# Attention's tail in another order: the last two reciprocal roots among GpSimd's scatters, row copies on ScalarE, the second image's norm ahead of the first's choice

## The reference, cut to what matters

```python
t = t + attn(layernorm(t))                     # 16 images x 256 tokens, 128 wide
z = layernorm(t)                               # per token
top_logits, top_idx = top_k(z @ Wg, 2)         # 8 experts
top_w = softmax(top_logits)
out = sum over e of combine[:, e] * (silu(z @ W1[e]) @ W2[e])
t = t + out
```

## Time and profile before

| what | value |
|---|---|
| median of 3 runs | 693.43 us (691.05 to 696.36) |
| profiled execution: span from first to last instruction | 692.4 us |
| busy share of the span: TensorE, VectorE, ScalarE, GpSimd | 85%, 69%, 45%, 38% |
| mean granted TensorE clock | 0.922 |
| last attention matmul of chunk 7 ends, first expert matmul starts | 475.8 us, 508.3 us |
| last scatter into the expert table issued, landed | 502.3 us, 504.6 us |

### The profile page before, as it was taken

How to read it: one execution, slowest core, us unless ns; L and a number is a source line. 1 busy time by engine, 2 the same in 40 slices (tenths; PEclk the granted TensorE clock), 3 DMA queues, 4 the chain that set the end, 5 groups by cost and what they waited for, 6 DMA issues and landing times. The chain is left out here.

```text
span 692.4 us, 11255 instructions
## 1 busy us (share of the span) xinstructions
PE 591.9 (85%) x3564; PEld 510.7 (74%) x3564; DVE 475.0 (69%) x1227; ACT 311.5 (45%) x619; POOL 264.6 (38%) x332
## 2 busy tenths in 40 slices
PE   5999999749789999999999998985259999999910
PEld 4788888636488998989898898885148888888810
DVE  6887784765558678777868788674527667767715
ACT  3322311243345353444535354442048888888800
POOL 4245334467000100141414132337603666666660
PEclk9999999959789999999999999877569999999975
DMA  7995155749450405050323314001178777766109
GB/s 265 360 336 171 39 172 169 242 163 341 133 149 5 153 1 153 2 172 13 124 62 98 88 43 142 25 17 47 39 250 290 240 238 229 259 230 212 60 5 359
DMA packets 55225, 105.49 MB, mean 152 GB/s; under 512 B 8744, under 2 KB 21689, under 8 KB 55040
## 3 DMA queue, kind: packets, MB, share of 16 engines
q1 hardware_dynamic: 50176, 96.24, 42.0%
q0 software_dynamic: 4992, 8.54, 3.5%
HBM read 58.15 MB, written 48.42 MB: 154 GB/s over the span
## 5 line engine op out<-in xcount | busy, mean ns | idle before, releaser
L1600 PE MATMUL bank<-rvx,s_expd 128*128 128x96 f32 x1024 | 136.1, 279 | 0.4 <-ACT s_expd L1052 0.4
L1600 PEld LDWEIGHTS bank<-rvx,s_expd 128*128 128x128 f32 x1024 | 129.7, 198 | 2.7 <-ACT s_expd L1052 2.0
L1904 POOL DMA_INDIRECT y_slots<-virt,pad_l x92 | 96.2, 1046 | 73.0 <-DVE virt L1955 50.0
L1052 ACT ACTIVATE s_expd<-bank 128x512 f32<-128x512 f32 x128 | 75.4, 596 | 96.6 <-PE bank L1584 96.0
L1247 DVE TENSOR_REDUCE s_max<-bank 128x2 f32<-128x512 f32 x128 | 87.2, 689 | 39.0 <-PE bank L1563 38.1
L968 POOL DMA_INDIRECT x_slots<-rows,slot_of x64 | 63.5, 993 | 58.6 <-DVE rows L1375 41.5
L934 POOL TENSOR_TENSOR ln_rstd<-ln_var,power 128x4 f32<-128x4 f32 x17 | 17.4, 1025 | 176.8 <-DVE ln_var L1223 176.8
L1943 DVE TENSOR_TENSOR k_stack<-virt,k_stack 128x512 fp32r<-128x512 f32 x92 | 63.5, 690 | 25.5 <-ACT k_stack L1923 24.8
L61 PE MATMUL bank<-pad_h,u_h 128*128 128x512 f32 x144 | 59.9, 416 | 8.2 <-DVE pad_l L399 8.2
L1584 PE MATMUL bank<-q_stack,k_stack 100*128 100x256 f32 x256 | 60.9, 321 | 5.2 <-DVE q_stack L1265 5.2
L1923 ACT ACTIVATE k_stack<-virt 128x512 fp32r<-128x512 f32 x92 | 58.2, 633 | 10.3 <-PE bank L63 7.6
(11 more groups left out here) (255 smaller groups left out, 1217.4 us busy)
## 6 DMA issues: line engine op xcount, KB each, us to landing
x_slots<-blank SPq DMA_DIRECT2D x8, 2112.0 KB, 18.0
pad_h<-w_split SPq DMA_DIRECT2D x23, 512.0 KB, 4.3
q_stack<-w_split SPq DMA_DIRECT2D x23, 512.0 KB, 5.5
qk_rows<-qk SPq DMA_DIRECT2D x16, 512.0 KB
k_stack<-qk_rows SPq DMA_DIRECT2D x96, 64.0 KB, 2.6
q_stack<-qk_rows SPq DMA_DIRECT2D x48, 128.0 KB, 2.6
pad_l<-x_slots SPq DMA_DIRECT2D x23, 264.0 KB, 5.1
e_raw<-in_w SPq DMA_DIRECT2D x16, 256.0 KB, 3.0
```

Of the source, the lines that this page charges most:

```text
L1052: nc.scalar.activation(expd[:, s % 2].rearrange("p a i -> p (a i)"), ps_st[s % 2][:, :], ACT.Exp).then_inc(exp_done, 1)
L1600: last = pe.matmul(ps_pv[s // 4][:, at:at + RVW], expd[:, s % 2, a, i * P:(i + 1) * P], rvx[:, ring, 2 * b + a, :], start=(a == 0), stop=( ...
L1904: pool.indirect_dma_start(out=y_slots[:, :], out_offset=bass.IndirectOffsetOnAxis(ap=ids, axis=0), in_=y_rows[:, t % 2, j, :], in_offset=N ...
```

## The change

It touches the tail of the last chunk alone, and one instruction at the start of the experts.

- GpSimd: the power of A stands after the first scatter of chunk 6 instead of the fourth; the power of B after the fifth, with the remaining three behind it. The copies of the rows of A and B leave GpSimd's queue. The row numbers of all four tiles of A and B are written in one pair of instructions between the two powers, after a wait for chunk 5's scatters to land.
- ScalarE: takes the two row copies, after the same wait, and takes `share_exp` of A after B's rows are moved out and copied.
- VectorE: `add_attention` and `norm_stats` of B stand ahead of `route` part 0 of A, and normalise B between parts 0 and 1 of A.
- TensorE: the transpose of B's rows stands ahead of A's `rank`.
- ScalarE, experts: one silu of a 128x1 column ahead of the first `z_split`; its result isn't used.

```diff
@@ GpSimd
+        def number_rows(g, ring):
             for k in range(2):
-                ids = consts["y_row"][:, k, chunk_of(u) * G + at.start:chunk_of(u) * G + at.stop]
-                pool.tensor_copy(rows[:, ring, k, at, ID_AT:ID_AT + 1].bitcast(I32), ids.unsqueeze(2)
+                ids = consts["y_row"][:, k, g * G:(g + 1) * G]
+                pool.tensor_copy(rows[:, ring, k, :, ID_AT:ID_AT + 1].bitcast(I32), ids.unsqueeze(2)
                                  ).then_inc(rows_copied, 1)
+        def copy_rows(g, ring):
+            pool.wait_ge(z_ready, tail_norm(g) + 1)
+            pool.tensor_copy(rows[:, ring, 1, :, 0:P], rows[:, ring, 0, :, 0:P]).then_inc(rows_copied, 1)
+            number_rows(g, ring)
...
-            pool.wait_ge(rows_copied, 3 * u + 3)
+            pool.wait_ge(rows_copied, 3 * (chunk_of(u) + 1) + (u == IMAGE_B))
...
-        scatter(NCH - 2, 0, (0,))
+        scatter(NCH - 2, 0, (0,), (0,))
         rstd(tail_norm(IMAGE_A))
-        scatter(NCH - 2, 0, (1,))
+        scatter(NCH - 2, 0, (0,), range(1, G))
+        pool.wait_ge(scattered[1], 2 * G * 16 * (NCH // 2 - 1))
+        number_rows(NCH - 1, 1)
+        scatter(NCH - 2, 0, (1,), (0,))
         rstd(tail_norm(IMAGE_B))
-        copy_rows(IMAGE_A, 1)
+        scatter(NCH - 2, 0, (1,), range(1, G))
         scatter(IMAGE_A, 1)
-        copy_rows(IMAGE_B, 1)
         scatter(IMAGE_B, 1)
@@ ScalarE
+        def copy_rows(u):
+            at = tiles_of(u)
+            act.wait_ge(z_ready, tail_norm(u) + 1)
+            nc.scalar.activation(rows[:, 1, 1, at, 0:P], rows[:, 1, 0, at, 0:P], ACT.Copy).then_inc(rows_copied, 1)
+
         gate(NCH - 1, 1)
         keep_z2(IMAGE_A)
         keep_o(IMAGE_B)
         keep_logits(IMAGE_A, 1)
+        act.wait_ge(scattered[1], 2 * G * 16 * (NCH // 2 - 1))
+        copy_rows(IMAGE_A)
+        keep_z2(IMAGE_B)
+        copy_rows(IMAGE_B)
         share_exp(IMAGE_A)
-        keep_z2(IMAGE_B)
         keep_logits(IMAGE_B, 1)
         share_exp(IMAGE_B)
@@ VectorE
-        route(IMAGE_A, 1, 0)
-        route(IMAGE_A, 1, 1)
         add_attention(IMAGE_B)
         norm_stats(tail_norm(IMAGE_B), t2_kept, IMAGE_B)
+        route(IMAGE_A, 1, 0)
+        normalise_t2(IMAGE_B, 1)
+        route(IMAGE_A, 1, 1)
         route(IMAGE_A, 1, 2)
         place(IMAGE_A, 1, ps_s[0])
-        normalise_t2(IMAGE_B, 1)
@@ TensorE
         tail_out(IMAGE_B)
+        tail_turn_back(IMAGE_B, 1)
         rank(IMAGE_A, ps_s[0])
-        tail_turn_back(IMAGE_B, 1)
         tail_route(IMAGE_B)
@@ ScalarE, experts
+        nc.scalar.activation(hid[:, 0, 0:1], ident[:, 0:1], ACT.Silu)
         z_split(0)
```

More of the change, by code:

```diff
@@ L950, in _, with scatter @@
         rstd(1)
[L952 to L955, removed]
+        def number_rows(g, ring):
             for k in range(2):
-                ids = consts["y_row"][:, k, chunk_of(u) * G + at.start:chunk_of(u) * G + at.stop]
-                pool.tensor_copy(rows[:, ring, k, at, ID_AT:ID_AT + 1].bitcast(I32), ids.unsqueeze(2)
+                ids = consts["y_row"][:, k, g * G:(g + 1) * G]
+                pool.tensor_copy(rows[:, ring, k, :, ID_AT:ID_AT + 1].bitcast(I32), ids.unsqueeze(2)
                                  ).then_inc(rows_copied, 1)
-        def scatter(u, ring, halves=(0, 1)):
+        def copy_rows(g, ring):
+            pool.wait_ge(z_ready, tail_norm(g) + 1)
+            pool.tensor_copy(rows[:, ring, 1, :, 0:P], rows[:, ring, 0, :, 0:P]).then_inc(rows_copied, 1)
+            number_rows(g, ring)
+        def scatter(u, ring, halves=(0, 1), tiles=None):
             if u == 0:
                 pool.wait_ge(blanked, 16 * (NE + 1))
-            pool.wait_ge(rows_copied, 3 * u + 3)
+            pool.wait_ge(rows_copied, 3 * (chunk_of(u) + 1) + (u == IMAGE_B))
             pool.wait_ge(rows_ready, 2 * u + 2)
             for k in halves:
-                for j in numbers(u):
+                for j in (numbers(u) if tiles is None else tiles):
                     pool.indirect_dma_start(
```

## The result

| | before | changed |
|---|---|---|
| median of 10 runs | 693.62 us (689.77 to 696.36) | 688.62 us (685.51 to 691.06) |
| ratio of the runs, 95% interval | | 0.9931 (0.9909 to 0.9952) |
| profiled execution: span | 692.4 us | 684.4 us |

By the ratio the kernel became 4.8 us faster (3.3 to 6.3 by the interval); the two medians differ by 5.0. The two profiled spans differ by 8.0, and that is not the size of the change: 3.5 of it lies ahead of the first instruction that the change moves, and 0.6 behind the first expert matmul. So the stage is read from a mark of its own. T is the start of chunk 6's first scatter (475.20 before, 471.73 after). All that comes later is counted from it.

What follows compares the result with a forecast made beforehand. TensorE holds the largest share, but the changed stage was taken as bound by GpSimd's queue up to the last scatter. 692.4 - 4.1 = 688.3 us span, plus 1.0 from span to median, gives 689.3 us, range 686.2 to 692.6.

Steps and rivals of the forecast that it cites:

- Power of A: GpSimd, chunk 6: starts right after the first scatter, at 476.46 and not 480.20, 3.74 us earlier.
- the sum: Last scatter starts at 498.26 against 502.34, 4.1 us earlier; 692.4 - 4.1 = 688.3 us for the span.
- B's norm ahead of A's choice: VectorE: B's residual sum starts at 482.5 and not 487.69 us; B's variance is complete at 483.94.
- Power of B: GpSimd: runs from 484.02 to 485.07 us, after a 0.8 wait for B's variance, with 11 scatters behind it.
- GpSimd's queue takes the end over from VectorE: B's row numbers are ready at 493.7 us, but GpSimd reaches B's scatters only at 494.5, 0.8 later.
- Row copies on ScalarE: Moved off GpSimd, they cost between nothing and 0.39 us; taken as nothing, since ScalarE waits there anyway.
- Silu ahead of the experts: ScalarE's 1.28 us table load moves into idle time and gives nothing; 6% chance that it counts, 688.0 us.
- that rival: GpSimd and VectorE get in each other's way: scatters of 1.20 us give 691.9, of 1.289 give 692.9; 15%.
- Chunk 5's scatters: New waits for their landing cost nothing if landed by 474.8 us; 7% chance of landing late, 696.4 at 485.
- TensorE's slow stretch: Start of experts, 4.4 us at clock 0.50, expected unchanged; 12% chance that it shifts, giving 687.1 or 691.5 us.

Runs made afterwards that it cites:

- the second: Interval from timing the unedited changed kernel again against the kernel before: median of 5 runs 688.97 us against 694.31, ratio 0.9915 (0.9889 to 0.9942).
- fourteen profiles: The first profiles of both kernels and twelve more: eight of edited kernels, one of the changed kernel, three of the kernel before; T from 470.98 to 476.71 us.

## Why the prediction was right

- **Power of A.** Forecast at T + 1.26, measured 1.23; alone it gives 2.88. Right. Its length was mis-sized: 1.28 and not 1.05. The 0.23 runs through to the last scatter, 23.27 against the forecast's 23.06, so the stage gave 3.87 where the sum had 4.1.
- **B's norm ahead of A's choice.** B's variance was forecast at T + 8.74 and came at 8.96 (480.69), later by about that 0.23. The order alone loses 0.34, which the prediction's sum doesn't say. Taken one after another, the runs split the 3.87 so: 2.88 for the power of A alone (to T + 24.26); 0.44 for the order, the power of B's new place and the row numbers taken together (to 23.82, row copies back on GpSimd); 0.55 for the row copies. What the order gives within the 0.44 stays open.
- **Power of B.** The idle time in front of it was forecast as 0.8 and measured 1.32: the pair of number copies takes 0.33 and the gap behind it 0.15, where the sum took 0.39 and 0.49 from copies that stood elsewhere, and the scatter that follows 0.97 and not 1.05; B's variance came 0.22 later too. It changed nothing, as the wait ended with the variance.
- **GpSimd's queue takes over from VectorE.** Right: no wait ahead of B's first scatter, 0.55 for two copies put back, and the chain stays on GpSimd. The place where it takes over is A's rows, with a wait of 0.23 above the pitch (0.2 forecast): the experiment with one more scatter ahead of the power shows that only the eight scatters behind that point count.
- **Row copies on ScalarE** took 0.41 each, above the upper bound of 0.39, and cost nothing: the exponent waited for VectorE.
- **Silu ahead of the experts** gives nothing, as forecast. In the run without it TensorE was busy all through the load. The page "ScalarE: Activation LUTs" of the Trainium skill (What ACT_TABLE_LOAD costs) puts a switch of sets at 2.66 us with its drain. The trace agrees on the load itself, 1.28 us; the first silu starts 0.02 after it, so no drain shows behind it.
- **The rivals.** No scatter behind the power of B took more than 1.05, so the scatters don't suffer. The other half of that rival did happen, on a part the prediction did not look at: the power of A beside VectorE. Chunk 5's scatters made nothing wait: normalise A was released by the power. TensorE's slow stretch at the start of the experts was 4.0 us (503.6 to 507.6, clock 0.51) against 4.4; over all profiles 4 to 10 products ran slow there, 6 to 8 in those of the kernel before, 7 and 10 in the changed one's, so no shift by the change shows.
- **The time.** 688.62 against 689.3 forecast, a gain of 4.8 by the ratio where 4.1 was forecast. The stage's 3.9 lies inside the first interval (3.3 to 6.3) and just below the second (0.9942 of 694.31 is a gain of 4.0). With the same clock ahead of T the spans differ by 4.3. Whether the rest is chance is not settled: nothing that the change edits runs ahead of T, T shows both levels in both kernels, and fourteen profiles are too few to say that the levels come equally often.

## What to carry to other kernels

In a tail where engines wait for one another, a short instruction that others wait for belongs in front of a queue's bulk work, at the point where its operand arrives; count the bulk that then stands behind its own wait. Reorder both ends of such a handover together and look for the point where the chain changes engine: here VectorE's order by itself lost 0.34, though it is part of a change that gains. When single edits are worth less than the runs scatter, measure from a mark inside the profile that the edits can't move.

## What the runs showed of the hardware

The power of A takes 1.27 to 1.28 in all eight profiles where part 0 of `retrieve` runs beside it, and 1.04 to 1.05 where VectorE is idle (five profiles) or runs the reciprocal alone (one). The power of B took 1.04 to 1.07 in all fourteen, also beside part 0 of A's choice, whose products of two SBUF tensors are 128x16. In the kernel before, a scatter took 1.20 and not 0.96; the 128x256 product of part 0 began at 476.47, within 0.01 of it. It is the same in the other four profiles with that order (1.18 to 1.20). So a GpSimd instruction that began together with part 0's product took about 0.23 longer.

This is no rule for every product of that size. In the changed kernel another 128x256 product of two SBUF tensors begins 0.04 after a scatter, and the scatter takes its usual 0.96 (GpSimd's and VectorE's timelines):

```profile
475.78 0.96 POOL L970 DMA_INDIRECT x_slots<-rows,slot_of  x1 [0.30 <-issue]
```

```profile
475.82 0.43 DVE L1309 TENSOR_TENSOR prod<-prod,ret 128x256 f32<-128x256 f32 x1
```

The Trainium skill's page "SBUF — State Buffer" (Who interferes with whom) has a VectorE instruction with two SBUF inputs contend with a GpSimd instruction that reads SBUF. The power reads SBUF, and the trace agrees in the direction; what is added is less than the product's 0.36. No run tried the product and the reduction behind it one by one, and why one scatter was longer and the other not stays open.
